# Attention scores for two heads per matmul, with head masks written by DMAs, and a new order of TensorE's steps

## What is computed

```python
q = (x @ wq.T + bq).reshape(B, S, 16, 16)        # 16 heads of 16
k = (x @ wk.T + bk).reshape(B, S, 16, 16)
v = (x @ wv.T + bv).reshape(B, S, 16, 16)
scores = zeros(B, S, 16, S)
scores[window, window] = q_w . k_w * 16**-0.5    # 128-token windows, block diagonal
scores[gi, gi] += q_g . k_g * 16**-0.5           # 64 global tokens, one in 32
out = (softmax(scores) @ v) @ wo.T + bo          # zero scores take part in the softmax
x = layernorm(x + out)
x = layernorm(x + experts(x))                    # 8 experts, the one with the largest logit
```

## Time and profile before

| what | value |
|---|---|
| median of 3 runs | 443.8 us (443.44 to 444.05) |
| span of the profiled execution (first to last instruction) | 442.8 us |
| the profiled execution's own time | not listed apart from the three runs, which all lie within 0.6 to 1.3 us of the span |
| start to `scores` of window 1 | 37.6 us |
| `scores` of window 1 to those of window 31 | 37.6 to 290.1 us, 30 steps |
| from there to the end (mostly experts) | 152.7 us |

### The profile page before, as it was taken

How to read it: one execution, slowest core, us unless ns; L and a number is a source line. 1 busy time by engine, 2 the same in 40 slices (tenths; PEclk the granted TensorE clock), 3 DMA queues, 4 the chain that set the end, 5 groups by cost and what they waited for, 6 DMA issues and landing times.

```text
span 442.8 us, 14658 instructions
## 1 busy us (share of the span) xinstructions
PE 405.3 (92%) x5747; PEld 339.8 (77%) x5747; DVE 326.1 (74%) x796; ACT 250.6 (57%) x523; POOL 220.4 (50%) x301
## 2 busy tenths in 40 slices
PE   5899799999999999999999899988798998999991
PEld 4758678888888888888888778756577887777891
DVE  6785687758757757757759888563668998899785
ACT  3424665675575575575576576676663555544421
POOL 4361343464464464464464566435733485477540
PEclk9999999999999999999999999999989999999997
DMA  8663740000000000000020000000000011011004
GB/s 240 186 199 111 240 137 4 27 25 0 24 24 0 24 24 0 24 24 0 24 72 4 25 2 3 3 1 2 0 2 2 1 49 47 0 47 49 34 15 143
DMA packets 21720, 20.34 MB, mean 46 GB/s; under 512 B 3133, under 2 KB 21682, under 8 KB 21682
## 3 DMA queue, kind: packets, MB, share of 16 engines
q1 hardware_dynamic: 16900, 15.07, 10.9%
q10 hardware_dynamic: 4782, 4.75, 3.3%
HBM read 15.41 MB, written 4.41 MB: 45 GB/s over the span
## 4 chain that ended last, share of the span: by engine, by line
PE 52%; DVE 26%; ACT 9%; issue 8%; DMA 3%; ACTq 1%; DVEq 0%; POOL 0%; POOLq 0%
DVE row_max_t L1154 10%; PE ps L1461 7%; PE ps L1737 7%; PE ps L1424 7%; PE ps L1562 5%; PE ps L1384 5%; PE ps L1415 4%; PE ps L1438 3%; PE ps L1444 3%; ACT probs L847 3%; DVE k_part L1013 2%; ACT boundsT_t L858 2%; PE ps L1406 2%; DMA rows<-in_L_attn_x_dram 2%; ACT k_part L713 2%
## 5 line engine op out<-in xcount | busy, mean ns | idle before, releaser
L847 ACT ACTIVATE probs<-ps 128x1024 f32<-128x1024 f32 x64 | 62.1, 1022 | 68.2 <-PE ps L1428 68.2
L1154 DVE TENSOR_REDUCE row_max_t<-ps 128x16 f32<-128x2048 f32 x31 | 70.9, 2287 | 3.7 <-PE ps L1415 3.6
L1737 PE MATMUL ps<-w_part,hm_part 128*128 128x256 f32 x384 | 53.8, 289 | 1.8 <-DVE hm_part L1332 1.8
L1415 PE MATMUL ps<-k_part,q_part 32*128 32x128 f32 x1584 | 51.5, 274 | 3.1 <-issue 1.5
L1415 PEld LDWEIGHTS ps<-k_part,q_part 32*128 32x128 f32 x1584 | 46.9, 186 | 9.2 <-issue 7.0
L1562 PE MATMUL ps<-xh_parts,w_part 128*128 128x512 f32 x192 | 53.8, 416 | 0.0
L557 POOL TENSOR_TENSOR q_part<-qf,q_part 128x512 fp32r<-128x512 f32 x32 | 41.0, 1281 | 25.7 <-ACT q_part L695 25.7
L599 POOL TENSOR_TENSOR attn_t<-num_t,rden_t 128x256 f32<-128x256 f32 x32 | 20.0, 624 | 64.7 <-DVE rden_t L1185 64.7
L1737 PEld LDWEIGHTS ps<-w_part,hm_part 128*128 128x128 f32 x384 | 48.2, 190 | 4.8 <-DVE hm_part L1332 2.4
L788 ACT ACTIVATE ffn_rows<-ps,b1s 128x512 f32<-128x512 f32 x32 | 22.0, 687 | 42.2 <-PE ps L1562 34.1
L1562 PEld LDWEIGHTS ps<-xh_parts,w_part 128*128 128x128 f32 x192 | 34.7, 194 | 6.5 <-issue 0.6
(11 more groups left out here) (234 smaller groups left out, 906.4 us busy)
## 6 DMA issues: line engine op xcount, KB each, us to landing
table<-rest_sums SPq DMA_DIRECT2D x4, 1088.0 KB, 6.1
xs<-in_L_attn_x_dram SPq DMA_DIRECT2D x16, 256.0 KB, 2.8
rows<-in_L_attn_x_dram ACTq DMA_DIRECT2D x4, 1024.0 KB, 8.1
out_dram<-yout SPq DMA_DIRECT2D x6, 512.0 KB, 2.9
w<-in_L_ffn_W_dram SPq DMA_DIRECT2D x2, 256.0 KB, 7.6
w<-in_L_ffn_W_dram SPq DMA_DIRECT2D x1, 512.0 KB, 4.2
out_dram<-yout SPq DMA_DIRECT2D x2, 256.0 KB, 2.6
out_dram<-yout ACTq DMA_DIRECT2D x2, 256.0 KB, 2.8
```

Of the source, the lines that this page charges most:

```text
L847: act.activation(probs[:, 2 * h:2 * h + 2, :], ps[:, 2 * h:2 * h + 2, :], ACT.Exp).then_inc(probs_ready, 1)
L1154: dve.tensor_reduce(row_max[:], ps_all, op=ALU.max, axis=AX.X).then_inc(max_ready, 1)
L1415: last = mm(ps[:, u, (2 * c + a) * P:(2 * c + a + 1) * P], q_part[x][quad(u), s, c, a, :], k_part[y][quad(u), s, c, :], start=(i == 0), st ...
L1737: mm(y, hm_part[a][:, 1 - p, f, c * P:(c + 1) * P], w2_part[b][:, f, :], start=(f == 0 and i == 0), stop=False)
```

## The change

Queries and keys are now kept unmasked (`q_parts`, `k_parts`, high and low) and in addition masked by head (`q_mask`, `k_mask`). The heads are laid out by turns over the partitions, even partitions head 0 and odd ones head 1 (an identity with reordered columns does it when the weights are transposed), so that a DMA can write head a's rows with a partition step of 2. The masked tiles are zeroed once, by POOL, in the prologue. `scores` has the unmasked query as stationary operand and both heads' masked keys as moving operand; `turned_scores` has the unmasked key and the masked queries. `k_mask` holds one pair of windows, `q_mask` two.

```diff
+            def to_heads(masked, parts, done):
+                for a in range(2):
+                    sp.dma_start(masked[a:P:2, :, a].bitcast(fp32), parts[a:P:2].bitcast(fp32)).then_inc(done, 16)
+            def mask_queries(w, s):
+                sp.wait_ge(q_ready, w // 2 + 1)
+                need(sp, turned_scores_in_psum, w - 2)
+                to_heads(q_mask[:, :, :, s:s + 2], q_parts[:, :, s:s + 2], q_masked)
+            def mask_keys(w, s):
+                sp.wait_ge(k_ready, w // 2 + 1)
+                need(sp, scores_in_psum, w)
+                to_heads(k_mask[:], k_parts[:, :, s:s + 2], k_masked)
...
             def step(t, s, steady=False):      # SP
+                if s % 2 and live(t + 1, steady) and (steady or t > 1):
+                    mask_queries(t + 1, (s + 1) % SLOTS)
+                    mask_keys(t + 1, (s + 1) % SLOTS)
                 if s % 2 and live(t + 5, steady):
                     load_x(t + 5)
...
                     rest_to_table(0)
+                    mask_queries(2, 2)
+                    mask_keys(2, 2)
                     sp.wait_ge(g_sums_ready, 1)
```

```diff
-            def scores(s):
-                for c in range(KC):
-                    for a in range(2):
-                        for i, (x, y) in enumerate(SPLIT):
-                            for u in range(UNITS):
-                                last = mm(ps[:, u, (2 * c + a) * P:(2 * c + a + 1) * P], q_part[x][quad(u), s, c, a, :],
-                                          k_part[y][quad(u), s, c, :], start=(i == 0), stop=(i == 2), tile_position=(32 * u, 0))
+            def scores(s, masked):
+                for c in range(KC):
+                    for i, (x, y) in enumerate(SPLIT):
+                        for u in range(UNITS):
+                            last = mm(ps[:, u, 2 * c * P:(2 * c + 2) * P].rearrange("p (a n) -> p a n", a=2), q_part[x][quad(u), s, c, :],
+                                      masked[quad(u), y, :, c, :], start=(i == 0), stop=(i == 2), tile_position=(32 * u, 0))
...
             def step(t, s, steady=False):      # TensorE
                 if cur and (steady or t > 0):
                     need(pe, probs_ready, 2 * (t - 1))
-                    pe.wait_ge(q_ready, t + 1)
-                    pe.wait_ge(k_ready, t // 2 + 1)
-                    scores(s).then_inc(scores_in_psum, 1)
+                    pe.wait_ge(q_ready, t // 2 + 1)
+                    pe.wait_ge(k_masked, 32 * (t // 2 + 1))
+                    scores(s, k_mask[:, :, :, p]).then_inc(scores_in_psum, 1)
+                if ahead and p == 0 and (steady or t > 0):
+                    queries_of(t + AHEAD)
+                if live(t + 1, steady) and p:
+                    values_of(t + 1)
+                    second_values()
                 if pp:
                     ... weigh ...
-                if ahead and p == 0:
-                    queries_of(t + AHEAD)
-                if live(t + 1, steady) and p:
-                    values_of(t + 1)
-                if live(t + 3, steady) and p:
-                    turn_x(t + 3)
                 if prev:
+                    pe.wait_ge(q_masked, 32 * ((t - 1) // 2 + 1))
                     turned_scores((s + 3) % SLOTS).then_inc(turned_scores_in_psum, 1)
                 if pp:
                     turn_sums().then_inc(sums_in_psum, 1)
+                if ahead and p == 0 and (steady or t > 0):
+                    keys_of(t + AHEAD)
                 if old:
                     output_product(t - 3)
                 ... transpose of the bounds ...
-                if ahead and p == 0:
-                    keys_of(t + AHEAD)
-                if live(t + 1, steady) and p:
-                    second_values()
+                if live(t + 3, steady) and p:
+                    turn_x(t + 3)
                 if pp:
                     need(pe, residual_ready, t - 2)
                     pe.wait_ge(attn_ready, t - 1)
                     ... transposes of attn ...
```

More of the change, by code:

```diff
@@ L168, in windowed_attention_then_top1_experts @@
         sb("rest_of_k_part", [P, 2 * HID])
-        qf = sb("qf", [P, 2, KC, 2, P])
+        q_parts = sb("q_parts", [P, 2, SLOTS, KC, P], fp32r)
+        q_part = [q_parts[:, i] for i in range(2)]
         va = sb("va", [P, SLOTS, HEADS * VP])
@@ L859, in step @@
                     last.then_inc(boundsT_ready, 1)
+                if not steady and t == 0:
+                    queries_of(AHEAD, AHEAD)
+                    keys_of(AHEAD, AHEAD)
                 if not steady and t == NW - 3:
@@ L967, in _ @@
                                      ALU.is_lt, ALU.add)
+            dve.wait_ge(ld_qk, 32)
+            qk_heads = qk_loaded[:].rearrange("r (u c a m) -> r c u a m", u=QUADS, c=KC, a=2)
+            for c in range(KC):
+                for a in range(2):
+                    last = dve.tensor_copy(qk_rows[:, c * P:(c + 1) * P].rearrange("r (u m a) -> r a u m", a=2, m=DH)[:, a], qk_heads[:, c, :, a])
+            last.then_inc(qk_ordered, 1)
             def put_weight(i):
@@ L1027, in _ @@
             dve.wait_ge(qg_high_ready, 1)
-            dve.tensor_tensor(q_part[1][:, GSLOT], qf[:, 0], q_part[0][:, GSLOT].bitcast(fp32), ALU.subtract).then_inc(qg_ready, 1)
+            for c in range(KC):
+                last = dve.scalar_tensor_tensor(q_part[1][:, GSLOT, c, :], ps[:, 6, c * P:(c + 1) * P], bq_col[:, c:c + 1],
+                                                q_part[0][:, GSLOT, c, :].bitcast(fp32), ALU.add, ALU.subtract)
+            last.then_inc(qg_ready, 1)
             low_of_x(0)
@@ L1186, in step @@
                 early(4)
+                if older:
+                    dve.wait_ge(stats_ready, t - 3)
+                    dve.tensor_copy(row(stats, t - 4, 2), mean_var[:, p, :]).then_inc(moments_ready, 1)
                 early(5)
@@ L1659, in step @@
                     values_of_rest()
-                if ahead and p == 0:
-                    keys_of(t + AHEAD)
-                if live(t + 1, steady) and p:
-                    second_values()
+                if not steady and t == 0:
+                    keys_of(AHEAD)
+                if live(t + 3, steady) and p:
+                    turn_x(t + 3)
                 if pp:
@@ L1681, in _ @@
                                            vec_rows[:, c * P:(c + 1) * P], ident[0:NVEC, 0:NVEC])
-            last = nc.tensor.transpose(ps[:, 4, KC * NVEC:KC * NVEC + FC], b1_rows[:], ident[0:FC, 0:FC])
+            nc.tensor.transpose(ps[:, 4, KC * NVEC:KC * NVEC + FC], b1_rows[:], ident[0:FC, 0:FC])
+            pe.wait_ge(qk_ordered, 1)
+            for c in range(KC):
+                last = nc.tensor.transpose(ps[:, 4, KC * NVEC + FC + 2 * c:KC * NVEC + FC + 2 * (c + 1)],
+                                           qk_rows[:, c * P:(c + 1) * P], ident[0:2, 0:2])
             last.then_inc(vecT_in_psum, 1)
@@ L1709, in _ @@
             pe.wait_ge(q_ready, 1)
-            scores(0).then_inc(scores_in_psum, 1)
+            pe.wait_ge(k_masked, 32)
+            scores(0, k_mask[:, :, :, 0]).then_inc(scores_in_psum, 1)
             pe.wait_ge(consts_ready, 1)
```

191 lines of the change are left out of this document (101 added, 90 removed).

## The result

The changed kernel takes **463.15 us** (median of 4 runs, 461.21 to 464.46) against 443.65 for the kernel before (median of 4, 443.44 to 444.05): a ratio of 1.044, 95% interval 1.041 to 1.047. I had forecast 441.2, between 428 and 448. The profiled execution has a span of 459.5 us, 16.7 more than before; it is the fastest of the four (461.21 us), so that its trace holds 16.7 of the 19.5 us by which the medians differ.

What follows compares the result with a forecast made beforehand. Odd steps were taken as bound by one serial chain, even steps by TensorE. Terms -4.6 - 0.5 + 1.0 + 2.0 - 0.8 + 0.3 = -2.6 us gave 441.2 us, range 428 to 448.

Steps and rivals of the forecast that it cites:

- The score product: In each step, `scores` as 24 matmuls of 256 columns take 0.86 us in place of 1.50, saving 0.64.
- The third rival: Streaming bounds `scores`: they stay at 1.50 us, all 30 steps lose 0.64, about 457 us; chance 0.05.
- Odd step 7.48, even step 8.60: In the loop, odd steps get 0.44 us shorter, even ones 0.10 longer as the residual loses its cover; -4.6 us.
- The masks in the loop, 3.2 us and no wait: Two 256 KB `k_mask` DMAs take 3.2 us within the 6.6 us between `scores` of successive steps, so nothing waits.
- The second rival: Masked keys land too late in the loop: gain gone at 6.8 us, 454 us at 7.5; chance 0.12.
- POOL's clearing lies ahead of its first subtraction, beside DMA waits: In the prologue, POOL's zeroing of the masked tiles falls beside DMA waits; no term in the sum.
- The masks of windows 0 and 1 share the DMA engines with the 1024 KB loads of rows: Ahead of step 1, masks and row loads share the DMA engines: +0.3 us, between -1 and +3.
- The masks of windows 2 and 3, 1 MB, are behind it: In the prologue, masks queue behind the table's 1088 KB, so `scores` of window 2 start near 48: +2.0 us (0 to +5).
- The 0.8 us that steps 1 to 3 were to save: In the prologue, steps 1 to 3 save about 0.8 us.
- DVE extras: In steps 3 and 24 to 27, extra DVE work has less cover, queries coming 1.01 us earlier: +1.0 us (0 to +5).

## Why the prediction was wrong, by its steps

- **The score product: right.** 0.86 forecast, 0.91 from `scores` to the next product, 0.78 of weight loads for 24 against 1.42 for 48. The third rival, streaming as the bound, falls. The Trainium skill (TensorE: Matmul & The Clock Gate, section "Back-to-back issue gap") gives its formula for an isolated matmul. I had taken it as a rule for this stream, by which 1.50 would have stayed; it does not carry over to four row tiles in flight, and the measurement decides.
- **Odd step 7.48, even step 8.60: right.** Measured 7.56 and 8.53 to 8.59 (the odd step at the loop's back edge takes 7.92 to 7.97, as it took 8.32 to 8.36 before). That the residual loses its cover and ends the even step is shown by the swap, which gives it 1.5 us of queries as cover and takes 0.6 off, and by the keys put last, which do the same. The 19 steps between windows 5 and 24 gained 3.6 us; 19 x 0.17 are 3.2.
- **The masks in the loop, 3.2 us and no wait: right.** A DMA landed 2.5 us behind its issue (those of `k_mask` between 90 and 243 us: 2.4 to 3.3), the second one of a pair went out 0.6 later, and no step of the loop waited for one. The second rival falls.
- **"POOL's clearing lies ahead of its first subtraction, beside DMA waits", at nothing: wrong, 3.8 us.** POOL had the time; what I did not ask is whom a busy POOL holds. The trace of the kernel before would have told it, in its first 5 us, where three small instructions of DVE end with POOL's clearing of `va`:
```profile
2.84 1.81 POOL L550 MEMSET va<- 128x2048 f32 x1
3.03 1.67 DVE L946 TENSOR_SCALAR colbits<-cid 128x64 int32<-128x64 int32 x1
```
The Trainium skill's rule above speaks against this very edit, and I had not looked for it.
- **"The masks of windows 0 and 1 share the DMA engines with the 1024 KB loads of rows", +0.3 (-1 to +3): wrong in size, 4.6 us** and 0.7 behind it. The term held the right collision at too low a price. While the masks and 2 MB of rows were on their way together, the median DMA of `k_mask` took 8.1 us to land. The loads of rows stood there already before the change (two were issued at 19.74 us), and with the clearing in pieces the wait was no shorter, so the late start is not its cause. With rows behind the masks the wait was gone; with rows earlier it was 0.6 us in one trace and 2.7 and 2.8 in two others.
- **"The masks of windows 2 and 3, 1 MB, are behind it" (the table), +2.0 (0 to +5): mechanism right, 2.4 us of the 3.2 that the stretch lost.** The working has a slip: by its own figures the table moves 1088 KB in 4.1 us (6.1 less 2), so 1 MB needs 3.9 and not "about 3", and the term would have been near +3. Issued ahead of the table the masks cost nothing, at no price for the table. The 0.8 us that steps 1 to 3 were to save did not come: steps 1 and 2, that wait taken out, are no shorter than before.
- **"DVE extras", +1.0 (0 to +5): wrong in size, 8.7 us.** These are steps 3 and 4 (+3.5) and 25 to 28 (+5.2) against the kernel before, and they should have saved 0.17 each. I priced a lost cover of 1.01 us a step; five of the six waits were 1.3 to 1.75, and TensorE's clock fell behind four of them, which cost 5.7 us more. Moved to where DVE waits anyhow, the same instructions gave 14 us back.
- **The clock** was in no term. The earlier trace rows show it full, and I took a duration for a duration. Where it fell behind an added wait, the wait was worth up to twice its length. It did not always fall: behind waits in the same steps, of 1.1 to 1.6 us, it fell in the changed kernel and stayed full in the runs with rows behind the masks (steps 3 and 4), with queries and keys swapped, and with the keys last. What decides it no run here settles.

The range was wrong because the terms' own bounds were too narrow, and its upper end did not even add those. With all three at their upper bounds (+5, +5 and +3) the sum would have come to 450.9; 448 held one or the other at its bound, and the clearing stood at nothing. They had a common cause, work taken on in stages without slack, to each of which I had given one sentence.

## What to carry to other kernels

Read the prologue and the one-off steps with the same care as the loop: here the loop gained 3.6 us, and the stretches with one clearing, two badly ordered queues and a few one-off instructions lost 20.7. Work given to an idle engine is free only if that engine shares nothing with a busy one; cut it small, or put it where the other one waits. And before a product is moved up to directly behind another, ask what its old cover hid in the steps that are unlike the rest.

## What the runs showed of the hardware

- While POOL cleared 4096 columns (3.54 us), a DVE copy of 256 columns on two partitions took 3.45 us; between pieces of 256 columns four copies took 0.56 us in all. Beside the clearing of 2048 columns (5.75 to 7.68 us) a copy of 128x4 took 1.22 us, ending with it, while instructions of 128x1 ahead of that copy (L1001 to L1006) took 0.14 to 0.15 us each.
- A DMA of 256 KB from SBUF to SBUF with a partition step of 2 landed 2.5 us behind its issue; beside 2 MB of loads on another queue it was over 7.
- In the changed kernel TensorE's weight loads ran at the lower clock behind waits of 1.30, 1.38, 1.45 and 1.57 us (2.37 to 2.46 us for 1.49) and at full clock behind one of 1.75 us. Behind the waits of 0.5 and 0.8 us in the loop's steps they stayed at full clock. In the run with the keys last the clock stayed full behind waits of 1.40 and 1.30 us in the same steps 25 and 26, so the length of a wait alone does not tell.
